# A gated cross-attention and feed-forward stack on one core: the opening stage's order of turns, key projections and GpSimd work is changed

## The chip, the cores and the metric

The kernel runs on one core of a Trainium2 chip. The time is device microseconds of one execution. A kernel's time is the median of several executions.

## The reference

`x` is 2048 tokens by 256, the context is 1601 rows by 256 with a mask. Four layers follow each other, each added to `x` behind a gate `tanh(g)`:

```python
x = x + tanh(g_xattn[0]) * latent_attention(ctx, layernorm(x), mask)   # 16 heads of 64
x = x + tanh(g_ffn[0])   * expert_ffn(layernorm(x))                    # 8 experts, top 2
x = x + tanh(g_xattn[1]) * cross_attention(layernorm(x), ctx)          # 16 heads of 16
x = x + tanh(g_ffn[1])   * quantised_ffn(layernorm(x))
```

Only the first layer's opening is touched. Its queries are `layer_norm(layernorm(x)) @ Wq`. Its keys and values come from 2048 rows of x and 1601 rows of context, one behind the other, so from 3649 keys:

```python
q = ln_lat @ Wq
k, v = split(concat([layer_norm(ctx), ln_lat]) @ Wkv)
out = softmax(q @ k.T * scale, masked) @ v            # per head
return out @ Wout
```

## The kernel before, in words

**Tiling.** `stage_latent` computes the first layer. The keys lie as 29 tiles of 128 (16 of x, 13 of context), and also as 8 chunks of 512: 4 of x, and 4 of context of which the last has 128. Two heads are worked on at once, in 8 groups. A group has 4 blocks of 512 queries. A block in a group is a unit `w`: there are 32, each of 29 steps `t`.

**Two passes over the scores.** The softmax needs a maximum per query before its scores are computed exactly. `pair(n)` is a rough pass: TensorE multiplies the high halves of 128 queries by 512 keys for two heads, and VectorE takes the two maxima (line 598). A unit has 29 such pairs. After its 29th, `max_of` makes the negated maxima, TensorE turns them (`turn`), and `shift_of` makes from them the shift that is added in `scores(w, t)`. ScalarE takes the exponential in `weigh`, TensorE multiplies by the values in `values`, and GpSimd and VectorE add up the exponentials (`add`, lines 348 and 630). Pairs run 33 ahead of the steps (`lead` = 29 + 4), so the first 33 pairs stand in an opening loop with no steps beside them. After them the loop of units interleaves `pair(n)` and `scores(w, t)`.

**The opening.** It has these parts on each engine, each written out as a program of its own and held together by semaphores:

- VectorE measures the rows of x and context (line 653), aggregates (658), makes reciprocals of deviations that ScalarE computes (line 483), and normalises: `norm_x(b)` for 4 blocks of 4 tiles of x (line 692) and `norm_ctx(b)` for the 13 tiles of context (line 699). Each signals `normed`, eight in all. Then come `project(0, a.nx)` (the low half of the first block of queries, line 565) and the loop of 33 pairs, with `fill_ctx(b)` ahead of pairs 0, 4, 8 and 12 (line 709: a transposed row block of context is scaled and masked rows are filled).
- TensorE transposes normalised rows (`turn_rows(b)`, line 826, b = 0 to 3 for x and 4 to 7 for context, two halves c each), projects (`project`, lines 845 for keys and queries, 853 for values) and computes pairs (line 885).
- ScalarE evacuates the transposes of x as full numbers and high halves (`row_block(b)`, lines 501 and 506, for context only 506), evacuates projections (lines 437, 443, 450) and rounds the steps between keys two tiles apart (`step_high`, line 462).
- GpSimd makes the low halves: of the weights (line 398), of the rows (`row_low(n)`, line 364, n = 0 to 7 for x), of the steps (`step`, `step_low`, lines 376 and 383). `fill[c]` (line 404) prepares the masked rows.

**Jobs.** There are 20 projections for a group: 8 chunks of keys, 4 blocks of queries, 8 of values. For the first group `open_jobs` gives their order. The first five (keys 0, queries 0, keys 1, 2, 3) stand before the loop of pairs, the rest behind odd pairs by `job_after_pair`. Pair n needs key chunk n // 4 for n below 28.

**Banks.** Rows and projections of the opening share four PSUM banks in turn, in the order of `open_uses`. A use waits until the fourth before it has been read:

```python
def free_open(what):
    n = open_place[what]
    if n >= 4:
        for read in open_read(open_uses[n - 4]):
            pe.wait_ge(*read)
```

For a block of queries "read" means that VectorE has made its low half. ScalarE's full rows go through three staging buffers: `row` n waits for `rows_lo` of n - 2. A projection on TensorE waits for `rows_lo` of the row blocks that it reads. `fill_ctx` waits for the same count.

Of the kernel before, what the change touches and what calls it, by code (L numbers as in the profile page):

```python
# [8 lines left out]
ACT = mybir.ActivationFunctionType  # L9
# [5 lines left out]
DC = D // P  # L15
TOK = 2048
NX = TOK // P
# [68 lines left out]
class Latent:  # L86


    def __init__(self):
        self.groups, self.heads, self.head = 8, 2, 64  # L90
        self.nl, self.nt = NX, NX + NCT
        self.keys = self.nt * P
        self.q_scale, self.gate = 0.125, 0
        self.ring = 6
        self.units = self.groups * NU
        self.steps = self.units * self.nt
        self.blocks = QB // P
        self.full = 7
        self.lead = self.nt + 4
        self.kchunks = [(a, 512) for a in range(0, NX * P, 512)] + [(NX * P + a, min(512, CTXP - a)) for a in range(0, CTXP, 512)]  # L100
        self.nx = NX * P // 512
        self.tail_at, self.tail = 1536, CTX - 1536
        self.vgroups = [list(range(a, min(a + 4, self.nt))) for a in range(0, self.nt, 4)]
        self.nk, self.nkq, self.nv = len(self.kchunks), len(self.kchunks) + NU, len(self.vgroups)
        self.jobs = self.nkq + self.nv
        keys_x, keys_c = list(range(self.nx)), list(range(self.nx + NU, self.nkq))
        queries = list(range(self.nx, self.nx + NU))
        v = list(range(self.nkq, self.jobs))
        self.open_jobs = [keys_x[0], queries[0], keys_x[1], keys_x[2], keys_x[3], v[0], v[1], keys_c[0], v[2], keys_c[1], v[3],
                          keys_c[2], keys_c[3], queries[1], v[4], queries[2], v[5], queries[3], v[6], v[7]]  # L110
        self.job_after_pair = {2 * i + 1: job for i, job in enumerate(self.open_jobs[5:19])} | {NX + NCT - 1: self.open_jobs[19]}
        self.query_low_after = {20: queries[1], 24: queries[2], 28: queries[3]}
        turns = [(0, 7), (0, 23), (0, 27), (1, 1), (1, 5), (1, 7), (1, 23), (1, 27), (2, 1), (2, 3), (2, 5), (2, 7),
                 (2, 23), (2, 27), (3, 1), (3, 3), (3, 5), (3, 7), (3, 23), (3, 27)]
        self.job_at = {((g - 1) * NU + u) * self.nt + t: (g, i) for g in range(1, self.groups) for i, (u, t) in enumerate(turns)}
        self.apart = 2
        self.sums_at, self.invert_at, self.pieces, self.divide_at, self.out_at = 9, 12, 4, 16, (17, 19)
        self.last_pair, self.turn_at = 24, 25
        self.dve_tiles = [5, 7, 9, 15, 17]
        self.pool_tiles = [t for t in range(self.nt) if t not in self.dve_tiles]  # L120


def stage_latent(nc, m, x_in, ctx_in, gates_in, affine_in, w_in, wo_in, mask_in):
# [5 lines left out]
    with Semaphores(nc, "a0") as sem, ExitStack() as ctx:  # L129
# [66 lines left out]
        order_kq = [i for i in a.open_jobs if i < a.nkq]  # L196
        turns = 2 * DC * (NL // 4)
        cols = [min(4, NL - 4 * b) * P for b in range(NL // 4)] + [min(4, NCT - 4 * b) * P for b in range(-(-NCT // 4))]
        open_uses = [("rows", n) for n in range(4)] + [("proj", 0, i) for i in a.open_jobs[0:2]]
        open_uses += [("rows", 4), ("rows", 5), ("proj", 0, a.open_jobs[2]), ("rows", 6), ("rows", 7)]  # L200
        open_uses += [("proj", 0, i) for i in a.open_jobs[3:5]]
        for n in range(a.lead):
            if n % 4 == 0 and n // 4 < turns // (2 * DC):
                open_uses += [("rows", turns // 2 + DC * (n // 4) + c) for c in range(DC)]
            if n in a.job_after_pair:
                open_uses.append(("proj", 0, a.job_after_pair[n]))
# [81 lines left out]
        def staged(n):  # L288
            return full[:, n % 3 * QB:(n % 3 + 1) * QB]
# [35 lines left out]
        def _(pool):  # L325
# [68 lines left out]
            nc.gpsimd.memset(ones[:, :], 1.0).then_inc(zeroed, 1)  # L394
            pool.wait_ge(affine_loaded, 32)
            pool.wait_ge(wscale_set, 1)
            pool.wait_ge(w_first, 1)
            nc.gpsimd.tensor_tensor(w_lo[:, :], w_st[:, :], w_hi[:, :], ALU.subtract).then_inc(w_split, 1)
            for n in range(6):
                row_low(n)  # L400
            pool.wait_ge(mask_loaded, 32)
            pool.wait_ge(affine_edge, DC)
            for c in range(DC):
                nc.gpsimd.tensor_scalar(fill[c], valid_u8[:, :], to_first[:, c:c + 1], first_key[:, c:c + 1],
                                        ALU.mult, ALU.add).then_inc(affine_edge, 1)
            row_low(6)
            row_low(7)
            for b in range(a.nk - a.nx):
                row_low(8 + 2 * b)
                row_low(9 + 2 * b)  # L410
# [19 lines left out]
        def _(act):  # L430
# [58 lines left out]
            def half_twice(h):  # L489
                act.wait_ge(var2_done, h + 1)  # L490
                deviation(var2[:, 8 * h:8 * h + 8], std[:, 8 * h:8 * h + 8])

            def row_block(b):
                for c in range(DC):
                    n = DC * b + c
                    hi, at = (m.xh, b * QB) if n < turns // 2 else (m.ch, (b - NL // 4) * QB)
                    if n < turns // 2:
                        act.wait_ge(rows_turned, n + 1)
                        if n >= 3:
                            act.wait_ge(rows_lo, n - 2)  # L500
                        nc.scalar.activation(staged(n)[:, 0:cols[b]], open_bank(("rows", n))[:, 0:cols[b]], ACT.Identity,
                                             bias=gx[:, 1, c:c + 1], scale=gx[:, 0, c:c + 1]).then_inc(full_done, 1)
                        act.wait_ge(full_done, n + 1)
                    else:
                        act.wait_ge(filled, n - turns // 2 + 1)
                    nc.scalar.activation(hi[:, c, at:at + cols[b]], staged(n)[:, 0:cols[b]], ACT.Copy).then_inc(rows_hi, 1)

            act.wait_ge(gates_loaded, 16)
            nc.scalar.activation(m.tg[:, :], gates[:, :], ACT.Tanh)
# [5 lines left out]
            nc.scalar.activation(w_hi[:, :], w_st[:, :], ACT.Copy, scale=WSCALE)  # L515
            nc.scalar.activation(w_st[:, :], w_st[:, :], ACT.Copy, scale=WSCALE).then_inc(w_first, 1)
            half(1)
            half_twice(1)
            act.wait_ge(affine_loaded, 32)
            row_block(0)  # L520
            row_block(1)
            project(0, a.open_jobs[0])
            project(0, a.open_jobs[1])
            row_block(2)
            act.wait_ge(aggregated, NT)
            deviation(mv[:, NL:NT, 1], std[:, NL:NT])
            nc.scalar.activation(warm[:, :], eps[:, :], ACT.Exp)
            project(0, a.open_jobs[2])
            row_block(3)
            project(0, a.open_jobs[3])  # L530
            project(0, a.open_jobs[4])
            for b in range(NL // 4):
                row_block(NL // 4 + b)
                if b:
                    step_high(0, b - 1)
                for n in (4 * b + 1, 4 * b + 3):
                    project(0, a.job_after_pair[n])
            step_high(0, a.nx - 1)
            for n in range(16, a.lead):
                if n in a.job_after_pair:  # L540
                    project(0, a.job_after_pair[n])
                if n in (17, 19, 21, 23):
                    step_high(0, a.nx + NU + (n - 17) // 2)
            act.wait_ge(prep, 1)
            for w in range(a.units):
                g, u = divmod(w, NU)
# [12 lines left out]
        def _(dve):  # L559
# [164 lines left out]
            aggregate(8, 8)  # L724
            norm_x(1)
            first_norm(1)
            measure_ctx(0)
            second_norm(1)
            norm_x(2)
            norm_x(3)  # L730
            for b in range(1, len(ctx_loaded)):
                measure_ctx(b)
            aggregate(NL, NCT)
# [11 lines left out]
                norm_ctx(b)  # L745
            project(0, a.nx)
            for n in range(a.lead):
                if n % 4 == 0 and n // 4 < len(ctx_loaded):
# [44 lines left out]
        def _(pe):  # L793
# [164 lines left out]

            turn_rows(0)
            turn_rows(1)  # L960
            project(0, a.open_jobs[0])
            project(0, a.open_jobs[1])
            turn_rows(2)
            project(0, a.open_jobs[2])
            turn_rows(3)
            project(0, a.open_jobs[3])
            project(0, a.open_jobs[4])
            for n in range(a.lead):
                if n % 4 == 0 and n // 4 < len(ctx_loaded):
                    turn_rows(NL // 4 + n // 4)  # L970
                if n == NT + 1:
                    turn(0)
                pair(n)
                if n in a.job_after_pair:
                    project(0, a.job_after_pair[n])
            pe.wait_ge(prep, 1)
            for w in range(a.units):
                g, u = divmod(w, NU)
                for t in range(NT):
                    n = w * NT + t + a.lead  # L980
                    if t % 2 == 0:
# [1404 lines left out]
```

## Time and profile before

| | us |
|---|---|
| median of 3 runs | 3269.82 |
| lowest and highest | 3268.73, 3271.04 |
| the profiled execution, its own time | 3268.37 |
| its span in the trace | 3266.5 |

The span lies 1.9 us below the profiled execution's own time. Over the span TensorE's matmuls are busy for 2956.8 us (91%), VectorE for 2435.5 us (75%), GpSimd for 2101.2 us (64%) and ScalarE for 1801.1 us (55%). The opening takes the first 91 us, about 3% of the span, so these shares say little about it; it has to be read from the timeline of each engine in that stretch. A duration in the timeline reaches to an instruction's end; the next one of the same engine often starts some 0.08 us before that, so a repeated cost is read from start to start.

### The profile page before, as it was taken

What the parts mean: (1) busy time and instruction counts of PE and PEld (TensorE: products, weight loads), DVE (VectorE), ACT (ScalarE), POOL (GpSimd) and SP (SyncE); (2) the same over time, 40 slices, a digit from 0 to 9 for tenths busy, and PEclk for the clock granted to TensorE, in tenths of its full rate; (3) what the DMA queues carried; (4) which work ended last, traced back from release to release, by engine and by line L of the source; (5) the groups of instructions that cost most, each with busy time, mean ns of one, the idle gap of its engine ahead of it and who ended that gap; (6) DMA issues with size and microseconds to landing.
All of it is one profiled execution on the core that took longest, in us unless ns stands there. A gap on an engine that the chain in (4) does not pass through costs nothing. (4 is left out here: it accounts for less than half of the span.)

```text
span 3266.5 us, 53578 instructions
## 1 busy us (share of the span) xinstructions
PE 2956.8 (91%) x21712; PEld 1094.2 (33%) x21720; DVE 2435.5 (75%) x3023; ACT 1801.1 (55%) x2009; POOL 2101.2 (64%) x1000
## 2 busy tenths in 40 slices
PE   5899999999999999999999999998597799999977
PEld 3233333333333333333333333322454133333334
DVE  8777787677777778767777776782545888888878
ACT  4455555455445555555554555445433488888863
POOL 5787988898898888889879888989510111111022
PEclk9999999999999999999999999999698799999989
DMA  1000000000000000000000000000210100000000
GB/s 62 6 1 1 1 8 1 1 7 1 1 7 1 1 1 7 1 1 7 1 1 1 2 1 1 1 1 1 68 32 14 43 8 7 6 7 8 5 3 25
DMA packets 24615, 28.72 MB, mean 9 GB/s; under 512 B 6511, under 2 KB 21296, under 8 KB 24370
## 3 DMA queue, kind: packets, MB, share of 16 engines
q1 hardware_dynamic: 24370, 25.31, 2.6%
q8 instruction: 172, 2.82, 0.4%
q14 instruction: 73, 0.60, 0.1%
HBM read 17.42 MB, written 2.10 MB: 6 GB/s over the span
## 5 line engine op out<-in xcount | busy, mean ns | idle before, releaser
L348 POOL TENSOR_TENSOR a_acc<-a_acc,a_prob 128x1024 f32<-128x1024 f32 x704 | 1725.3, 2451 | 297.7 <-ACT a_prob L480 216.0
L598 DVE TENSOR_REDUCE a_part_max<-wide 128x2 f32<-128x1024 f32 x880 | 1069.1, 1215 | 443.1 <-PE wide L885 442.3
L480 ACT ACTIVATE a_prob<-slot,a_mask_bias 128x1024 f32<-128x1024 f32 x928 | 986.9, 1113 | 738.6 <-PE slot L914 721.7
L929 PE MATMUL bank<-a_prob,a_val 128*64 128x512 f32 x3712 | 897.1, 605 | 2.1 <-ACT a_prob L480 2.1
L1218 ACT ACTIVATE a_prob<-slot,a_mask_bias 128x1024 f32<-128x1024 f32 x416 | 455.2, 1115 | 67.0 <-PE slot L1418 53.9
L885 PE MATMUL wide<-a_k_hi,a_q_hi 64*128 64x512 f16 (+1 forms) x2016 | 352.4, 362 | 113.8 <-DVE a_part_max L598 106.0
L1262 DVE TENSOR_REDUCE a_part_max<-wide 128x1 f32<-128x512 f32 x514 | 333.5, 684 | 37.6 <-PE wide L1406 20.8
L929 PEld LDWEIGHTS bank<-a_prob,a_val 128*64 128x64 f32 x3712 | 226.5, 136 | 394.0 <-issue 289.4
L914 PE MATMUL slot<-a_q_hi,a_k_lo 64*128 64x512 f16 x1856 | 352.4, 376 | 0.0
L914 PE MATMUL slot<-a_q_hi,a_k_step_hi 64*128 64x512 f16 x1728 | 327.9, 376 | 2.4 <-ACT a_prob L480 2.3
L914 PE MATMUL slot<-a_q_lo,a_k_step_hi 64*128 64x512 f16 x1728 | 327.7, 376 | 0.0
L885 PEld LDWEIGHTS wide<-a_k_hi,a_q_hi 64*128 64x128 f16 x2016 | 90.2, 93 | 550.2 <-DVE a_part_max L598 444.6
L1432 PE MATMUL bank<-a_prob,a_val 128*32 128x256 f32 x3328 | 262.8, 392 | 0.1
L1178 POOL TENSOR_TENSOR x_res<-a_gated,x_res 128x512 f32<-128x512 f32 x32 | 41.2, 1287 | 342.5 <-ACT a_gated L1230 342.5
L630 DVE TENSOR_TENSOR a_acc<-a_acc,a_prob 128x1024 f32<-128x1024 f32 x96 | 217.4, 2264 | 6.4 <-ACT a_prob L480 6.4
L1406 PE MATMUL wide<-a_k_op,a_q_op 48*128 48x512 f16 (+1 forms) x686 | 166.5, 355 | 36.5 <-DVE a_part_max L1262 29.0
L1262 DVE TENSOR_REDUCE a_part_max<-bank 128x1 f32<-128x512 f32 x254 | 173.6, 684 | 16.0 <-PE wide L1406 14.1
L1418 PE MATMUL slot<-a_q_op,a_k_op 64*128 64x512 f16 x832 | 160.9, 383 | 3.6 <-DMA a_q_op<-a_shift 2.3
L1166 POOL CAST a_hi<-a_y 128x512 f16<-128x512 f32 x15 | 9.2, 611 | 225.8 <-ACT a_y L1207 225.8
L636 DVE RECIPROCAL bank<-bank 128x128 f32<-128x128 f32 x128 | 120.8, 948 | 36.6 <-PE bank L937 36.6
L914 PEld LDWEIGHTS slot<-a_q_hi,a_k_lo 64*128 64x128 f16 x1856 | 90.5, 94 | 110.2 <-issue 0.5
L1406 PE MATMUL bank<-a_k_op,a_q_op 48*128 48x512 f16 (+1 forms) x338 | 109.6, 354 | 15.9 <-DVE a_part_max L1262 14.4
(397 smaller groups left out, 3274.7 us busy)
## 6 DMA issues: line engine op xcount, KB each, us to landing
a_w_staged<-in_w SPq DMA_DIRECT2D x8, 384.0 KB, 3.2
x_res<-in_x SPq DMA_DIRECT2D x4, 512.0 KB, 5.8
a_q_op<-a_hi SPq DMA_DIRECT2D x128, 16.0 KB, 1.8
out_x<-x_res SPq DMA_DIRECT2D x16, 128.0 KB, 1.7
a_k_op<-mid_k_hi SPq DMA_DIRECT2D x32, 52.0 KB, 2.2
mid_context<-in_ctxt SPq DMA_DIRECT2D x1, 1601.0 KB, 6.7
mid_w_staged<-in_w1a SPq DMA_DIRECT2D x4, 384.5 KB, 6.5
a_acc<-in_ctx SPq DMA_DIRECT2D x3, 512.0 KB, 8.4
```

Of the source, the lines that this page charges most:

```text
L348: nc.gpsimd.tensor_tensor(acc, before, prob[:, k % R, :], ALU.add).then_inc(added_p, 1)
L480: nc.scalar.activation(prob[:, k % R, :], m.slot[k % 2][:, :], ACT.Exp, bias=mbias[:, t:t + 1]).then_inc(probs_ready, 1)
L598: nc.vector.reduce_max(part_max[:, w % 2, :, j, c], pairs, AX.X).then_inc(max_used, 1)
L630: nc.vector.tensor_tensor(acc, before, prob[:, k % R, :], ALU.add).then_inc(added_v, 1)
L885: ins = nc.tensor.matmul(out, qh[g % 2][r, q0:q0 + P], src, start=True, stop=True, tile_position=(h * HALF, 0))
L914: ins = nc.tensor.matmul(score_bank(w, t, h), left, right, start=(whole and n == 0), stop=(n == len(terms) - 1), tile_position=(h * HALF, ...
L929: ins = nc.tensor.matmul(av[r, :], val[g % 2][:, t, r], prob[:, k % R, h * QB:(h + 1) * QB], start=(t == 0), stop=(t == NT - 1), tile_posi ...
L1218: nc.scalar.activation(prob[:, k % R, :], slot(("scores", w, s))[:, :], ACT.Exp, bias=mbias[:, t:t + 1]).then_inc(probs_ready, 1)
L1262: nc.vector.reduce_max(part_max[:, w % 2, 2 * z + h, j:j + 1, c], src, AX.X).then_inc(ring_used, 1)
L1406: ins = nc.tensor.matmul(bank(("max", n, h))[:, at:at + width_k], q_op[z][r, u * QB + j * P:u * QB + (j + 1) * P], k_op[g][z][r, k0:k0 + w ...
L1418: ins = nc.tensor.matmul(slot(("scores", w, s))[:, h * QB:(h + 1) * QB], k_op[g][z][r, t * P:(t + 1) * P], q_op[z][r, u * QB:(u + 1) * QB] ...
L1432: ins = nc.tensor.matmul(av[r, q], val[g][:, t, r], prob[:, (k + h // 2) % R, c0 + q.start:c0 + q.stop], start=(n == 0), stop=(n == a.halv ...
```

## The change

- TensorE turns rows 0, 1, 2 of x, projects keys 0, turns rows 3, projects queries 0, and goes to the loop. Keys 1, 2 and 3 are projected behind pairs 1, 3 and 5. The first block of context is turned and filled ahead of pair 2, the others ahead of pairs 6, 10, 14. The remaining jobs have places of their own, some behind pairs that follow each other.
- The order in which the banks are used follows. The first block of queries now has place 9 and not 5.
- ScalarE does the rows of x singly: row 0 ahead of the second square root, rows 4 and 5 around the deviation of context, rows 6 and 7 behind both first projections. It rounds steps at places of their own (`step_after`).
- GpSimd waits for `normed` 4 (all of x normalised) before its first two low halves and the low half of the weights, then makes rows 2 and 3, waits for `normed` 8 (context normalised), then does `fill` and rows 4 to 7.
- VectorE measures two tiles of the first context block where it measured four, and the other two behind `norm_x(3)`.
- In the first unit `scores(0, 0)` stands before `pair(33)` and not behind it.

```diff
+        self.job_after_pair = {1: keys_x[1], 3: keys_x[2], 5: keys_x[3], 7: keys_c[0], 9: v[0], 11: keys_c[1], 13: v[1], 14: queries[1],
+                               15: keys_c[2], 17: v[2], 18: v[3], 19: keys_c[3], 21: queries[2], 22: v[4], 23: v[5], 25: queries[3],
+                               27: v[6], 28: v[7]}
+        self.step_after = dict(zip((6, 9, 13, 16, 18, 20, 22, 24), keys_x + keys_c))
+        self.open_jobs = [keys_x[0], queries[0]] + list(self.job_after_pair.values())
+        self.query_low_after = {17: queries[1], 24: queries[2], 28: queries[3]}
...
+        open_uses = [("rows", n) for n in range(6)] + [("proj", 0, a.open_jobs[0])] + [("rows", 6), ("rows", 7)]
+        open_uses.append(("proj", 0, a.open_jobs[1]))
         for n in range(a.lead):
-            if n % 4 == 0 and n // 4 < turns // (2 * DC):
+            if n % 4 == 2 and n // 4 < turns // (2 * DC):
...
             pool.wait_ge(affine_loaded, 32)
             pool.wait_ge(wscale_set, 1)
+            pool.wait_ge(normed, NL // 4)
+            row_low(0)
+            row_low(1)
             pool.wait_ge(w_first, 1)
             nc.gpsimd.tensor_tensor(w_lo[:, :], w_st[:, :], w_hi[:, :], ALU.subtract).then_inc(w_split, 1)
-            for n in range(6):
-                row_low(n)
+            row_low(2)
+            row_low(3)
+            pool.wait_ge(normed, len(cols))
             pool.wait_ge(mask_loaded, 32)
             pool.wait_ge(affine_edge, DC)
             for c in range(DC):
                 nc.gpsimd.tensor_scalar(fill[c], valid_u8[:, :], to_first[:, c:c + 1], first_key[:, c:c + 1],
                                         ALU.mult, ALU.add).then_inc(affine_edge, 1)
-            row_low(6)
-            row_low(7)
+            for n in range(4, 8):
+                row_low(n)
...
             half(1)
+            act.wait_ge(affine_loaded, 32)
+            row(0)
             half_twice(1)
-            act.wait_ge(affine_loaded, 32)
-            row_block(0)
+            row(1)
             row_block(1)
+            row(4)
+            act.wait_ge(aggregated, NT)
+            deviation(mv[:, NL:NT, 1], std[:, NL:NT])
+            row(5)
+            nc.scalar.activation(warm[:, :], eps[:, :], ACT.Exp)
             project(0, a.open_jobs[0])
             project(0, a.open_jobs[1])
-            row_block(2)
...
             row_block(3)
...
             turn_rows(0)
             turn_rows(1)
+            turn_rows(2)
             project(0, a.open_jobs[0])
+            turn_rows(3)
             project(0, a.open_jobs[1])
-            turn_rows(2)
-            project(0, a.open_jobs[2])
-            turn_rows(3)
-            project(0, a.open_jobs[3])
-            project(0, a.open_jobs[4])
...
+                    if w == 0 and t == 0:
+                        scores(w, t)
+                        pair(n)
+                        continue
```

## Rows read from the trace of the kernel before

**Rows 1.** Busy time of each engine by stretch, with the granted clock.
```profile
22.80:24.00 1.20, 1.20 (x4) 0.46 (x3) 1.20 (x2) 0.23 (x1) 1.20 (x2) 0.50 0.00 0
39.00:46.20 7.20, 6.37 (x26) 3.76 (x27) 0.01 (x1) 4.24 (x7) 2.31 (x2) 0.70 0.00 0
46.20:91.30 45.10, 33.61 (x313) 18.69 (x311) 44.39 (x46) 18.36 (x37) 29.19 (x28) 0.96 0.02 3
1000.00:1700.00 700.00, 666.73 (x4374) 233.93 (x4372) 520.87 (x478) 366.13 (x414) 600.85 (x250) 1.00 0.01 2
```
The columns are: stretch, its length, busy time and count of PE, PEld, DVE, ACT and POOL, granted clock, DMA share, GB/s.

**Rows 2.** Waits in the first 92 us: total, times, longest.
```profile
PE slot L826 <- DVE a_q_lo L565: 10.2, 1, 10.2
DVE a_k_full L709 <- PE slot L826: 7.7, 3, 7.3
```

**Rows 3.** VectorE's timeline in the opening: start, us, then the instruction.
```profile
12.35 2.70 DVE L692 TENSOR_SCALAR a_prob<-x_res,a_mv,a_rstd 128x256 f32<-128x256 f32 x4
15.52 1.35 DVE L692 TENSOR_SCALAR a_prob<-x_res,a_mv,a_rstd 128x256 f32<-128x256 f32 x4
19.04 6.17 DVE L692 TENSOR_SCALAR a_prob<-x_res,a_mv,a_rstd 128x256 f32<-128x256 f32 x8
25.13 3.03 DVE L653 BATCH_NORM_STATS2 a_stats<-a_acc 128x6 f32<-128x256 f32 x9
28.07 0.96 DVE L658 BATCH_NORM_AGGREGATE a_mv<-a_stats 128x2 f32<-128x6 f32 x13
31.21 7.08 DVE L699 TENSOR_SCALAR a_acc<-a_acc,a_mv,a_rstd 128x256 f32<-128x256 f32 x13
38.20 0.69 DVE L565 SCALAR_TENSOR_TENSOR a_q_lo<-slot,a_q_hi 128x512 f16<-128x512 f32 x1
46.19 0.75 DVE L709 SCALAR_TENSOR_TENSOR a_k_full<-slot,a_affine_c,a_prob 128x512 f32<-128x512 f32 x1 [7.30 <-PE slot L826]
...
47.52 1.22 DVE L598 TENSOR_REDUCE a_part_max<-wide 128x2 f32<-128x1024 f32 x1
48.65 1.22 DVE L598 TENSOR_REDUCE a_part_max<-slot 128x2 f32<-128x1024 f32 x1
...
89.91 1.22 DVE L598 TENSOR_REDUCE a_part_max<-wide 128x2 f32<-128x1024 f32 x1
```

**Rows 4.** GpSimd's timeline in the opening.
```profile
12.85 1.72 POOL L398 TENSOR_TENSOR a_w_lo<-a_w_staged,a_w_hi 128x768 f16<-128x768 f32 x1 [10.72 <-ACT a_w_staged L516]
19.10 0.19 POOL L362 COPY a_first_key<-a_k_full 128x1 f32<-128x1 f32 x1 [4.53 <-ACT xt_hi L506]
...
20.89 3.52 POOL L364 TENSOR_TENSOR xt_lo<-a_k_full,xt_hi 128x512 f16<-128x512 f32 x3
28.67 1.15 POOL L364 TENSOR_TENSOR xt_lo<-a_k_full,xt_hi 128x512 f16<-128x512 f32 x1 [4.25 <-ACT xt_hi L506]
31.14 3.46 POOL L404 TENSOR_SCALAR a_prob<-a_valid_u,a_to_first,a_first_key 128x1664 f32<-128x1664 uint8 x2
79.92 0.43 POOL L383 TENSOR_TENSOR a_k_lo<-a_k_step,a_k_step_hi 128x128 f16<-128x128 f32 x1 [1.48 <-ACT a_k_step_hi L462]
```

**Rows 5.** ScalarE's timeline, one row block's start to the next.
```profile
17.62 0.76 ACT L501 ACTIVATE a_k_full<-slot,a_affine_x 128x512 f32<-128x512 f32 x1
...
18.95 0.76 ACT L501 ACTIVATE a_k_full<-slot,a_affine_x 128x512 f32<-128x512 f32 x1
```

**Rows 6.** TensorE's timeline: a cold projection's part, a warm one's, and the first scores.
```profile
23.30 1.06 PE L845 MATMUL slot<-xt_hi,a_w_lo 128*128 128x512 f16 x2
44.26 0.59 PE L845 MATMUL slot<-xt_hi,a_w_hi 128*128 128x512 f16 x2 [0.80 <-issue]
91.66 0.66 PE L914 MATMUL slot<-a_q_hi,a_k_hi 64*128 64x512 f16 x2
93.36 0.66 PE L914 MATMUL slot<-a_q_hi,a_k_hi 64*128 64x512 f16 x2
94.77 0.39 PE L885 MATMUL wide<-a_k_hi,a_q_hi 64*128 64x512 f16 x2
```

More of the change, by code:

```diff
@@ L108, in __init__ @@
         v = list(range(self.nkq, self.jobs))
[L109 to L112, printed above, removed]
+        self.job_after_pair = {1: keys_x[1], 3: keys_x[2], 5: keys_x[3], 7: keys_c[0], 9: v[0], 11: keys_c[1], 13: v[1], 14: queries[1],
[4 more added lines that the diff above has]
+        self.query_low_after = {17: queries[1], 24: queries[2], 28: queries[3]}
         turns = [(0, 7), (0, 23), (0, 27), (1, 1), (1, 5), (1, 7), (1, 23), (1, 27), (2, 1), (2, 3), (2, 5), (2, 7),
@@ L198, in stage_latent @@
         cols = [min(4, NL - 4 * b) * P for b in range(NL // 4)] + [min(4, NCT - 4 * b) * P for b in range(-(-NCT // 4))]
-        open_uses = [("rows", n) for n in range(4)] + [("proj", 0, i) for i in a.open_jobs[0:2]]
-        open_uses += [("rows", 4), ("rows", 5), ("proj", 0, a.open_jobs[2]), ("rows", 6), ("rows", 7)]
-        open_uses += [("proj", 0, i) for i in a.open_jobs[3:5]]
+        open_uses = [("rows", n) for n in range(6)] + [("proj", 0, a.open_jobs[0])] + [("rows", 6), ("rows", 7)]
+        open_uses.append(("proj", 0, a.open_jobs[1]))
         for n in range(a.lead):
-            if n % 4 == 0 and n // 4 < turns // (2 * DC):
+            if n % 4 == 2 and n // 4 < turns // (2 * DC):
                 open_uses += [("rows", turns // 2 + DC * (n // 4) + c) for c in range(DC)]
@@ L491, in half_twice, with row @@
                 deviation(var2[:, 8 * h:8 * h + 8], std[:, 8 * h:8 * h + 8])
+            def row(n):
+                b, c = divmod(n, DC)
+                hi, at = (m.xh, b * QB) if n < turns // 2 else (m.ch, (b - NL // 4) * QB)
+                if n < turns // 2:
+                    act.wait_ge(rows_turned, n + 1)
+                    if n >= 3:
+                        act.wait_ge(rows_lo, n - 2)
+                    nc.scalar.activation(staged(n)[:, 0:cols[b]], open_bank(("rows", n))[:, 0:cols[b]], ACT.Identity,
+                                         bias=gx[:, 1, c:c + 1], scale=gx[:, 0, c:c + 1]).then_inc(full_done, 1)
+                    act.wait_ge(full_done, n + 1)
+                else:
+                    act.wait_ge(filled, n - turns // 2 + 1)
+                nc.scalar.activation(hi[:, c, at:at + cols[b]], staged(n)[:, 0:cols[b]], ACT.Copy).then_inc(rows_hi, 1)
             def row_block(b):
                 for c in range(DC):
[L495 to L506, printed above, removed]
+                    row(DC * b + c)
             act.wait_ge(gates_loaded, 16)
@@ L517, in _ @@
             half(1)
+            act.wait_ge(affine_loaded, 32)
+            row(0)
             half_twice(1)
-            act.wait_ge(affine_loaded, 32)
-            row_block(0)
+            row(1)
             row_block(1)
+            row(4)
[3 more added lines that the diff above has]
+            nc.scalar.activation(warm[:, :], eps[:, :], ACT.Exp)
             project(0, a.open_jobs[0])
             project(0, a.open_jobs[1])
-            row_block(2)
-            act.wait_ge(aggregated, NT)
-            deviation(mv[:, NL:NT, 1], std[:, NL:NT])
-            nc.scalar.activation(warm[:, :], eps[:, :], ACT.Exp)
-            project(0, a.open_jobs[2])
-            row_block(3)
-            project(0, a.open_jobs[3])
-            project(0, a.open_jobs[4])
[L532 to L539, printed above, removed]
+            row_block(3)
+            for n in range(a.lead):
+                if n % 4 == 2 and n // 4 < len(ctx_loaded):
+                    row_block(NL // 4 + n // 4)
                 if n in a.job_after_pair:
                     project(0, a.job_after_pair[n])
-                if n in (17, 19, 21, 23):
-                    step_high(0, a.nx + NU + (n - 17) // 2)
+                if n in a.step_after:
+                    step_high(0, a.step_after[n])
             act.wait_ge(prep, 1)
@@ L726, in _ @@
             first_norm(1)
-            measure_ctx(0)
+            dve.wait_ge(ctx_loaded[0], 16)
+            measure(rows(0, 2), NL, 2)
             second_norm(1)
@@ L730, in _ @@
             norm_x(3)
+            measure(rows(0, 4)[:, 2:4, :], NL + 2, 2)
             for b in range(1, len(ctx_loaded)):
@@ L747, in _ @@
             for n in range(a.lead):
-                if n % 4 == 0 and n // 4 < len(ctx_loaded):
+                if n % 4 == 2 and n // 4 < len(ctx_loaded):
                     fill_ctx(n // 4)
@@ L960, in _ @@
             turn_rows(1)
+            turn_rows(2)
             project(0, a.open_jobs[0])
+            turn_rows(3)
             project(0, a.open_jobs[1])
-            turn_rows(2)
-            project(0, a.open_jobs[2])
-            turn_rows(3)
-            project(0, a.open_jobs[3])
-            project(0, a.open_jobs[4])
             for n in range(a.lead):
-                if n % 4 == 0 and n // 4 < len(ctx_loaded):
+                if n % 4 == 2 and n // 4 < len(ctx_loaded):
                     turn_rows(NL // 4 + n // 4)
```

## The prediction

> **What bounds the kernel now.** I first split the span into stretches by busy time. In steady state TensorE is busy for 667 of 700 us, but in the first 91 us it is not the bound [rows 1]. There VectorE's timeline sets the pace: one chain of normalising up to 38.9, a hole, then 33 pairs of maxima to 91.1 (the last starts at 89.91 and takes 1.22). In the stretch from 46.2 VectorE is busy for 44.4 of 45.1 us [rows 1, 3]. Everything in the units comes behind that last pair: the first scores start at 91.66 [rows 6]. So the opening's end is the date to move, and each microsecond there should move all that follows.
>
> Two things in the opening are seen to be wasted. The waits name the first: TensorE stood for 10.2 us until VectorE had made the first queries' low half at 38.9, because bank place 9 (rows 6 of x) waits for place 5, those queries. After it came the last turns of x, keys 2 and 3 and the turns of context; VectorE waited 7.3 us for those before its fill at 46.19 [rows 2, 3].
>
> The second is in VectorE's own durations. Four normalising instructions took 1.35 us at 15.52, but 2.70 at 12.35 and 6.17 for eight at 19.04; thirteen took 7.08 at 31.21 [rows 3]. The slow ones are those beside GpSimd: its weight subtract starts at 12.85, its row subtracts at 19.10, its fill of 3.46 us at 31.14 [rows 4]. Undisturbed one costs 0.32 us (1.35 less an overlap of 0.08, by four). In the last group 11 undisturbed ones leave 3.5 us for two, about 1.73 each, which is one of GpSimd's two fills (3.46 by two).
>
> **The pause of GpSimd.** The first four norms save 1.35 us and the eight of blocks 2 and 3 save 6.17 - 2.70 = 3.5. Two statistics moved behind them save another 0.65 (3.03 us for nine is 0.33 each). So norm_x(3) ends 5.5 us earlier, at 19.7 and not 25.2 [rows 3]. Its turns come in time, as the first two blocks' normalising ends earlier as well. Then VectorE has 11 statistics (3.6) and 13 aggregates (0.9): 24.2.
>
> GpSimd starts at 19.8. Rows 0 and 1 with their small copies took 20.89 - 19.10 + 1.17 = 3.0, the weights 1.7, rows 2 and 3 take 1.17 each [rows 4]: 22.8, 24.5, 26.8. ScalarE's row 4 waits for the second of these, 22.8, and takes 1.33 [rows 5], so the deviation of context behind it runs at 24.3, just in time. The few small operations before the context norms can meet GpSimd's rows 2 and 3, so I let the norms start only at 26.9. Thirteen at 0.32 to 0.33 end at 31.1 instead of 38.3: 7.2 us gained.
>
> What nothing in the trace shows is a statistic beside a GpSimd instruction; here 11 run beside it. The nearest row is the aggregates: 13 in 0.96 us, the last of them beside the subtract that starts at 28.67, with no slowing [rows 3, 4]. I take 0. The other end is that each is held as a norm is, one for each GpSimd instruction of about 1.2 us: six get through by 26.8, and the other five, the aggregates and the small operations push the norms' start by 3.3 us. A gain from below nothing is excluded, since they had no company before.
> The Trainium skill (SBUF — State Buffer, its section on what contends) says that a VectorE instruction with at most one SBUF input and outside the two-port modes does not contend with GpSimd, while one in a two-port mode is fully blocked by a GpSimd instruction that started first. By it the statistics cost 0; the 1.73 us of a blocked norm agree with the second half, and no row here shows the first half for statistics.
>
> **What the pause makes late.** The weights' low half comes at 24.5 and not 14.6, and the first projection with it. SP's load of the second group's weights stands behind that signal; those weights are used after the last opening projection, so this costs nothing. A projection of six matmuls of 512 columns costs 2.6 us at the lower clock (0.50 granted, 0.43 us for each) and 1.3 at the higher (0.22 each) [rows 1, 6]. TensorE is idle before 24.5, so keys 0 is cold: 27.1. Turns of rows 3 take it to about 28, queries 0, between the two prices, to 30.1, their high half to 30.7. VectorE's low half follows at 31.1 and ends at 31.8; even a cold projection shifts this by a microsecond that falls into the hole below. Pairs 0 and 1 take 1.13 each start to start [rows 3]: 34.1.
>
> GpSimd now does its fills only after 31.1: 34.6. Rows 4, 5, 6 follow at 35.8, 36.9 and 38.1. The first fill_ctx halves wait for the counts 6 and 7, that is 36.9 and 38.1. So VectorE gets a new hole of 2.8 us at 34.1, and the fill ends at 38.1 + 0.67 = 38.8 (0.67 from 46.19 to 47.52 for two) [rows 3, 4]. Behind the same queue ScalarE's row 7 waits for count 5 (35.8) and holds the evacuation of keys 1 until about 38; pair 4 needs it at 41. TensorE's turn of the second context half waits for row 7's full numbers (36.5), ready by 37.5. Neither ends later than GpSimd.
>
> **The pair loop.** Before, the first context fill ended at 47.5 with no pair done; now it ends at 38.8 with two. From there the loop holds the same VectorE work: 91.1 - 8.7 - 2 x 1.13 = 80.1. To be added are gaps by TensorE. It has three more projections there, and jobs behind successive pairs (13 to 15, 17 to 19, 21 to 23). With a job behind every pair its cycle is 1.3 + 0.3 for the pair against VectorE's 1.13, a deficit of 0.45 us a pair; the two banks of pairs hide part and VectorE's fills and low halves more. I take 0.3 for each of three runs and 0.6 for keys 2 and 3, which may still be cold: 1.5. Bounds: 0, and 11 jobs at 0.5, 5.5. The loop ends at 81.6, 9.5 us earlier.
>
> **Scores before pair 33.** scores(0, 0) needs the shift, ready 2.3 us before the last pair ends, and no longer waits behind pair 33. Before, scores of two steps lay between 91.66 and 94.77; now only the second does, about 1.7 us cold. The gain is 1.4 (94.77 - 93.36), at most 1.7 [rows 6].
>
> **Sum.** 9.5 + 1.4 = 10.9 us. The profiled execution took 3268.4 around a span of 3266.5; minus 10.9 that is 3257.5. The median of the runs lies 1.4 above that execution, so I forecast 3258.9.
>
> **Rivals.**
> Statistics held by GpSimd: 3.3 us of the pause's gain go back, and the fills move with it. 3262.2. For it speaks only that no row shows the case.
> TensorE late throughout the loop: gaps of 5.5 in place of 1.5 give 3262.9. For it: three runs of jobs; against it: 33.6 us of TensorE work in a stretch of 45 [rows 1].
> The gain is taken back by the first unit (a wait for the last low step, or for values, or VectorE and GpSimd meeting differently): 3269.8. The low steps ended at 80.35, 11.3 us ahead of the first scores [rows 4, 6]; they too move forward, with at least 7 us left by my count, so this speaks against it.
> Slower by the clock: TensorE is idle at 34 to 36.5 and could stay at 1.2 GHz through the loop. Its work there is 33.6 + 3.9 for the three keys = 37.5 us; doubled, the loop would run from 32 to 107, and the time would be about 3284. Cover is 12 us, so the gain is gone once 23 of the 37.5 us run at the low clock, and it is slower by 0.2% from about 30. Against it: granted 0.96 in that stretch before, though it too began after an idle time (0.70 in the 7 us ahead) [rows 1].
>
> **How the numbers follow.** The forecast has 0.79, statistics 0.06, late TensorE 0.06, taken back 0.06, the clock 0.03. Its own range is 3255 to 3262: no gaps and 1.7 for the scores give 3257.1, and 2 us each way stand for how the first unit falls in. With two rivals the range is 3254 to 3264.5. A measurement here tells about 0.2%, 6.5 us, from no change: faster needs less than 3263.3. Forecast, statistics and half of late TensorE with a little of its rest give 0.90; same 0.07; slower 0.03.
>
> **What would show it.** Norms at 0.32 us throughout blocks 0 to 3 and the last of context near 31; w_lo ending near 24.5; a hole in VectorE from about 34 to 37, with the fill released by GpSimd's rows; no wait of 10 us in TensorE for the low queries; the last pair of 33 ending near 81.6, the first scores some 2 us before it. The forecast fails if the statistics stretch, if holes of over half a microsecond stand before many pairs, or if the first unit is longer by what the opening lost.

## The result and the profile after

The changed kernel took 3258.18 us (median of 6, 3255.98 to 3260.7) beside 3270.98 us (median of 6, 3268.73 to 3274.95) for the kernel before. The ratio is 0.9962 with a 95% interval of 0.9949 to 0.9974: between 8.5 and 16.7 us faster. The profiled execution took 3259.05 us with a span of 3257.3, against 3268.37 and 3266.5 before.

VectorE's timeline in the changed opening (start, us, then the instruction) answers to [rows 3]:

```profile
12.27 1.38 DVE L694 TENSOR_SCALAR a_prob<-x_res,a_mv,a_rstd 128x256 f32<-128x256 f32 x4
17.03 2.68 DVE L694 TENSOR_SCALAR a_prob<-x_res,a_mv,a_rstd 128x256 f32<-128x256 f32 x8
19.62 3.69 DVE L655 BATCH_NORM_STATS2 a_stats<-a_acc 128x6 f32<-128x256 f32 x11
23.22 0.95 DVE L660 BATCH_NORM_AGGREGATE a_mv<-a_stats 128x2 f32<-128x6 f32 x13
...
24.29 1.20 DVE L740 CAST a_mcol<-a_mcol_u 128x13 f32<-128x13 uint8 x1
25.66 0.94 DVE L746 TENSOR_TENSOR a_rstd<-a_rstd,a_mcol 128x13 f32<-128x13 f32 x1
26.64 4.29 DVE L701 TENSOR_SCALAR a_acc<-a_acc,a_mv,a_rstd 128x256 f32<-128x256 f32 x13
30.84 0.68 DVE L567 SCALAR_TENSOR_TENSOR a_q_lo<-slot,a_q_hi 128x512 f16<-128x512 f32 x1
...
36.85 0.75 DVE L711 SCALAR_TENSOR_TENSOR a_k_full<-bank,a_affine_c,a_prob 128x512 f32<-128x512 f32 x1 [3.06 <-POOL xt_lo L365]
37.95 0.75 DVE L711 SCALAR_TENSOR_TENSOR a_k_full<-slot,a_affine_c,a_prob 128x512 f32<-128x512 f32 x1 [0.35 <-POOL xt_lo L365]
38.62 1.22 DVE L600 TENSOR_REDUCE a_part_max<-wide 128x2 f32<-128x1024 f32 x1
...
80.82 1.22 DVE L600 TENSOR_REDUCE a_part_max<-wide 128x2 f32<-128x1024 f32 x1
```

Every norm of x and context now costs 0.32 to 0.33 us from start to start; the last eight of x took 6.17 us before and take 2.68. The context norms end at 30.9 instead of 38.3. The new hole is where it was looked for, 3.06 + 0.35 us, and its releaser is GpSimd. The loop of pairs ends at 82.04 (80.82 + 1.22) instead of 91.13.

GpSimd's timeline (answers to [rows 4]) shows the two pauses and the queue that sets the hole:

```profile
22.71 1.63 POOL L402 TENSOR_TENSOR a_w_lo<-a_w_staged,a_w_hi 128x768 f16<-128x768 f32 x1
24.31 2.26 POOL L365 TENSOR_TENSOR xt_lo<-a_k_full,xt_hi 128x512 f16<-128x512 f32 x2
31.04 3.44 POOL L409 TENSOR_SCALAR a_prob<-a_valid_u,a_to_first,a_first_key 128x1664 f32<-128x1664 uint8 x2 [4.47 <-DVE a_acc L701]
34.44 4.50 POOL L365 TENSOR_TENSOR xt_lo<-a_k_full,xt_hi 128x512 f16<-128x512 f32 x4
```

TensorE's timeline (answers to [rows 6]) shows the swapped scores: the first score matmul stands at 79.92, before the last pair's maxima are out, and pair 34 at 84.20.

```profile
79.92 0.61 PE L918 MATMUL slot<-a_q_hi,a_k_hi 64*128 64x512 f16 x2
82.09 0.61 PE L889 MATMUL wide<-a_k_hi,a_q_hi 64*128 64x512 f16 x2 [0.29 <-DVE a_part_max L600]
82.50 0.63 PE L918 MATMUL slot<-a_q_hi,a_k_hi 64*128 64x512 f16 x2
84.20 0.63 PE L889 MATMUL wide<-a_k_hi,a_q_hi 64*128 64x512 f16 x2
```

To see whether the gain is passed on, I take one instruction that stands once in each unit, the negated maxima. First the third and the last of the kernel before, then those of the changed kernel:

```profile
218.40 0.21 DVE L609 TENSOR_REDUCE a_neg_max<-a_part_max 128x8 f32<-128x64 f32 x1
...
2215.88 0.22 DVE L609 TENSOR_REDUCE a_neg_max<-a_part_max 128x8 f32<-128x64 f32 x1
```

```profile
208.11 0.21 DVE L611 TENSOR_REDUCE a_neg_max<-a_part_max 128x8 f32<-128x64 f32 x1
...
2206.72 0.22 DVE L611 TENSOR_REDUCE a_neg_max<-a_part_max 128x8 f32<-128x64 f32 x1
```

The lead is 10.3 us at the third and 9.2 at the last; the spans differ by 9.2. So the opening's gain goes through the first layer nearly one to one, and in this pair of executions through the rest of the program too. That last part is not sure to a microsecond: from the last unit's negated maxima to the end of the span, where no version changes anything, the ten traces of this document took between 1047.1 and 1050.9 us (the kernel before and the changed one both 1050.6). So a difference of up to 3.8 us between single executions can come from there, and I read the experiments at the loop's end and at the units' maxima first.

### The profile page after: what moved, and what is told of

It is laid out like the page before. It is cut to its first block and busy times, and to the rows that moved or that the text cites. A ratio compares the mean times of both kernels' runs of the same rounds, so it can differ in the third digit from the quotient of the medians.

```text
span 3257.3 us, 53578 instructions
## 1 busy us (share of the span) xinstructions
PE 2957.0 (91%) x21712; PEld 1093.0 (34%) x21720; DVE 2430.7 (75%) x3023; ACT 1800.9 (55%) x2009; POOL 2099.9 (64%) x1000
## 5 line engine op out<-in xcount | busy, mean ns | idle before, releaser
L1411 PE MATMUL bank<-a_k_op,a_q_op 48*128 48x512 f16 (+1 forms) x338 | 109.8, 355 | 15.9 <-DVE a_part_max L1267 14.4
```

Source lines behind the costliest of these rows:

```text
L1411: ins = nc.tensor.matmul(bank(("max", n, h))[:, at:at + width_k], q_op[z][r, u * QB + j * P:u * QB + (j + 1) * P], k_op[g][z][r, k0:k0 + w ...
```

## The experiments

Each kernel's time is compared with the kernel before as it was run beside it ("before beside it"), in the ratio of the medians. "Loop end" is the end of the 33rd pair's maxima in the profiled execution.

| kernel | us | before beside it | ratio, 95% interval | loop end |
|---|---|---|---|---|
| before | | | | 91.13 |
| changed | 3258.18 | 3270.98 | 0.9962, 0.9949 to 0.9974 | 82.04 |
| changed, no pause | 3263.82 | 3269.02 | 0.9983, 0.9975 to 0.9992 | 87.98 |
| before, pause only | 3274.09 | 3269.02 | 1.0014, 1.0005 to 1.0023 | 94.65 |
| before, low half first | 3263.64 | 3269.02 | 0.9981, 0.9972 to 0.9990 | 87.24 |
| changed, pair 33 first | 3259.18 | 3269.02 | 0.9971, 0.9959 to 0.9982 | 82.87 |
| changed, fills on ScalarE | 3254.4 | 3270.33 | 0.9952, 0.9939 to 0.9964 | 79.24 |
| changed, second pause out | 3261.38 | 3270.33 | 0.9974, 0.9963 to 0.9984 | 85.48 |
| before, swap only | 3267.31 | 3269.44 | 0.9994, 0.9985 to 1.0003 | 92.30 |
| fills on ScalarE, jobs spaced | 3251.6 | 3269.44 | 0.9947, 0.9935 to 0.9960 | 78.14 |

**The changed kernel without the pause.**

```diff
-            pool.wait_ge(normed, NL // 4)
-            row_low(0)
-            row_low(1)
             pool.wait_ge(w_first, 1)
...
-            row_low(2)
-            row_low(3)
-            pool.wait_ge(normed, len(cols))
+            for n in range(6):
+                row_low(n)
```

> The changed kernel with GpSimd's order of before (weights' low half as soon as it can, rows 0 to 5, fill, rows 6 and 7) and both waits for the normalising taken out. Theory (the pause is worth about 4 us, because its saving of 7 us is partly given back in GpSimd's late rows): the norms take 2.7, 6.2 and 7.1 us again, the context norms end near 38.3 instead of 30.9, no hole stands before the first context fill, the loop of pairs ends near 85.9 instead of 82.0, time about 3262. Rival (the pause is worth nothing, the turns alone made the gain): the loop ends within 1 us of 82, 3258. Rival (the pause is worth all of the 7 us): 3265.

Measured: VectorE's norms, and the first context fill of this kernel:

```profile
19.32 5.19 DVE L690 TENSOR_SCALAR a_prob<-x_res,a_mv,a_rstd 128x256 f32<-128x256 f32 x8
29.91 9.48 DVE L697 TENSOR_SCALAR a_acc<-a_acc,a_mv,a_rstd 128x256 f32<-128x256 f32 x13
...
42.17 0.73 DVE L707 SCALAR_TENSOR_TENSOR a_k_full<-bank,a_affine_c,a_prob 128x512 f32<-128x512 f32 x1
```

The theory's mechanism holds, its size was short by 2 us. The context norms took 9.48 us and not 7.1, because rows 5, 6 and 7 of GpSimd also fell beside them; they ended at 39.4 and not at 30.9. The fill had no hole before it, so 3.4 us of these 8.5 are given back there. The pause is worth 5.9 us at the loop's end; the rest of the change is 3.2 us there, and it is faster than before by 0.8 to 2.5 thousandths. The first rival (the pause is worth nothing) is out. The second (all of 7 us, 3265) is not: the median of 3263.82 lies nearer to it than to the theory's 3262, and 5.9 lies nearer to 7 than to 4. Only the hole and the norms in the trace say that part of the saving goes back.

**The kernel before with the pause alone.** The same GpSimd lines as in the change, nothing else.

> The kernel before with GpSimd's two pauses and new order alone; turns, projections and ScalarE as before. Theory (the pause needs the new order of turns): the first projections start near 24.5, the deviation of context waits on ScalarE behind them until 33, context norms end near 38, the wait of TensorE for the queries' low half stays, and GpSimd's fills and rows come after it, so that the first context fill ends near 50 instead of 47.5: about 2.8 us slower than before. Rival (the saving on VectorE is a gain by itself): 4 to 7 us faster than before.

Measured: slower, by 1.6 to 7.5 us; 5.1 by the medians and 3.5 at the loop's end, where 2.8 were expected. Its norms of x were as quick as in the changed kernel (2.67 us for eight). VectorE then stood twice:

```profile
DVE a_k_full L713 <- PE slot L830: 10.0, 1, 10.0
DVE a_rstd L743 <- ACT a_std L487: 8.2, 1, 8.2
```

ScalarE's deviation of context, which the second wait is for:

```profile
33.91 0.29 ACT L487 ACTIVATE a_std<-a_mv,a_eps 128x13 f32<-128x13 f32 x1
```

The deviation of context stands behind the first projections on ScalarE, and these wait for the weights' low half. So the 5 us saved in the norms were waited away, and the first fill started at 49.72. The rival falls: a quicker VectorE was no gain by itself. Two things of the old order stood in its way, the deviation behind the projections (8.2 us) and the bank wait for the low queries (10.0 us, with GpSimd's fills and rows 4 to 7 behind the late norms). The changed kernel has neither. No run has the pause with only one of them mended, so how much each is needed for the pause to pay is argued from the waits and not shown.

**The kernel before with one instruction moved.**

```diff
+            project(0, a.nx)
             dve.wait_ge(mask_loaded, 32)
             nc.vector.tensor_scalar(mbias[:, NL:NT], mcol_u8[:, :], -1.0, -MASKED, ALU.add, ALU.mult).then_inc(prep, 1)
...
             for b in range(len(ctx_loaded)):
                 norm_ctx(b)
-            project(0, a.nx)
```

> The kernel before with one move on VectorE: the first queries' low half is made ahead of the context norms and not behind them. Theory (the 7.3 us hole was that one wait on bank place 5): TensorE turns rows 6 and 7 near 30, projects keys 2 and 3 by 39.5, the first context fill ends near 41.9 instead of 47.5, time 5.7 us below the kernel before. Rival (the hole was TensorE's and ScalarE's amount of work and not the wait): less than 2 us.

Measured: 5.4 us faster by the medians, 3.9 at the loop's end. VectorE's timeline:

```profile
28.91 0.66 DVE L565 SCALAR_TENSOR_TENSOR a_q_lo<-slot,a_q_hi 128x512 f16<-128x512 f32 x1
...
31.69 8.75 DVE L699 TENSOR_SCALAR a_acc<-a_acc,a_mv,a_rstd 128x256 f32<-128x256 f32 x13
40.78 0.75 DVE L709 SCALAR_TENSOR_TENSOR a_k_full<-slot,a_affine_c,a_prob 128x512 f32<-128x512 f32 x1 [0.34 <-PE slot L826]
...
67.92 1.23 DVE L598 TENSOR_REDUCE a_part_max<-wide 128x2 f32<-128x1024 f32 x1 [1.61 <-PE wide L885]
```

The hole of 7.3 us is down to 0.34, so it was the wait on bank place 5, whose release stood at the end of VectorE's queue. The context norms grew from 7.08 to 8.75 us, since row subtracts of GpSimd that had waited now ran beside them. The fill came 5.4 us earlier; 1.6 of that is lost again at 67.92, where VectorE waits for a pair that stands behind a projection of queries. TensorE did this projection at 1.2 GHz (granted clock 0.50 from 64.73 to 67.41, and 1.00 from 60.00 to 64.19, ahead of it).

**The swap of the first scores, both ways.** In the changed kernel the four lines of the swap were taken out; in the kernel before they were put in.

> The changed kernel with pair(33) ahead of scores(0, 0) again. Theory: the loop of pairs ends at 82.0 as before, pair 34 comes 1.5 us later, time about 1.5 us above the changed kernel. Rival (the first unit hides it): no difference, and pair 34's delay is gone by the second unit.

> The kernel before with scores(0, 0) ahead of pair(33) and nothing else. Theory (the swap is worth what the comparison of traces showed for it, 1.2 us, in any order of the opening): the loop of pairs ends at 91.1 as before, the maxima of the third unit (218.4 before) come 1.2 to 1.5 us earlier, time 1 to 1.5 us below the kernel before, too little to be sure of by the times. Rival (its effect lies in how the clock rises in the changed opening): the third unit's maxima within 0.3 us of 218.4.

Measured: the times can't settle it (3259.18 with 3269.02 beside it, 3258.18 with 3270.98 beside it; 0.9994 with an interval over 1). The openings of two executions also differ by about a microsecond with nothing changed ahead of the swap (82.04 and 82.87; 91.13 and 92.30), so the sign that was expected, the date of the third unit's negated maxima, came out at 0.5 us in the kernel before with the swap. I read the stretch from the loop's end to these maxima in place of it, a choice made after the result. The third unit's rows, first without the swap in the changed kernel, then with it in the kernel before:

```profile
210.44 0.21 DVE L611 TENSOR_REDUCE a_neg_max<-a_part_max 128x8 f32<-128x64 f32 x1
```

```profile
217.90 0.21 DVE L609 TENSOR_REDUCE a_neg_max<-a_part_max 128x8 f32<-128x64 f32 x1
```

The stretch is 127.3 us in the kernel before (218.40 - 91.13) and 125.6 with the swap; it is 126.1 in the changed kernel and 127.6 without the swap. That is 1.5 to 1.7 us, but not all of it is the swap. The stretch in all ten traces, beside TensorE's granted clock in the first 8 us behind the loop's end:

| kernel | swap | granted clock | stretch |
|---|---|---|---|
| fills on ScalarE, jobs spaced | yes | 1.00 | 125.4 |
| before, swap only | yes | 0.96 | 125.6 |
| changed, no pause | yes | 0.92 | 125.6 |
| changed | yes | 0.79 | 126.1 |
| changed, fills on ScalarE | yes | 0.54 | 127.4 |
| changed, second pause out | yes | 0.51 | 127.6 |
| before | no | 0.79 | 127.3 |
| changed, pair 33 first | no | 0.75 | 127.6 |
| before, low half first | no | 0.73 | 127.7 |
| before, pause only | no | 0.71 | 127.8 |

With the swap the stretch runs from 125.4 to 127.6 us and follows the clock. At the same clock, 0.79, it is 126.1 with the swap and 127.3 without: by this one pair of traces the swap itself is worth 1.2 us, and the other 0.3 to 0.5 us of both comparisons go with a higher clock. So the rival of the clock fits in part, and the other one, that the first unit hides the swap, is out: pair 33 first is still 2.3 us behind the changed kernel at the last unit's maxima (2209.01 and 2206.72). Its span is as short all the same, 3257.0 against 3257.3, because its later layers took 2.6 us less.

**The second pause taken out.** Only `pool.wait_ge(normed, len(cols))` is removed from the changed kernel.

> The changed kernel without GpSimd's second pause (it no longer waits for the context norms before its fills; the first pause and the order stay). Theory (a norm beside a GpSimd instruction is held until that ends, one for each): two norms of 1.7 us, three of 1.2, the context norms end near 36.3 instead of 30.9, no hole follows, the first context fill ends near 40.6 instead of 38.6: 2 us slower than the changed kernel. Rival (the fills taken off the chain are worth more than the slower norms): 1 to 2 us faster.

Measured: 3.4 us later at the loop's end (expected 2). VectorE's norms and GpSimd beside them:

```profile
26.71 10.45 DVE L700 TENSOR_SCALAR a_acc<-a_acc,a_mv,a_rstd 128x256 f32<-128x256 f32 x13
...
39.94 0.73 DVE L710 SCALAR_TENSOR_TENSOR a_k_full<-bank,a_affine_c,a_prob 128x512 f32<-128x512 f32 x1
```

```profile
26.63 3.47 POOL L408 TENSOR_SCALAR a_prob<-a_valid_u,a_to_first,a_first_key 128x1664 f32<-128x1664 uint8 x2
30.06 4.68 POOL L365 TENSOR_TENSOR xt_lo<-a_k_full,xt_hi 128x512 f16<-128x512 f32 x4
```

GpSimd had six instructions beside the norms and not five. Seven free norms at 0.33 and six that last as long as GpSimd's instructions (3.47 + 4.68 = 8.15) give 10.5, which is the 10.45 measured. Waiting is right here: the second pause costs GpSimd about 4.5 us and saves VectorE 6.2.

**The fills moved to ScalarE.**

```diff
+            def fill_one(c):
+                act.wait_ge(mask_loaded, 32)
+                act.wait_ge(affine_edge, DC)
+                nc.scalar.activation(fill[c], valid_u8[:, :], ACT.Identity, bias=first_key[:, c:c + 1],
+                                     scale=to_first[:, c:c + 1]).then_inc(affine_edge, 1)
...
+            fill_one(0)
             row(5)
...
-            row_block(3)
+            row(6)
+            fill_one(1)
+            row(7)
```

> The changed kernel with both fills of masked rows made by ScalarE (one ahead of row 5, one ahead of row 7) and not by GpSimd; nothing else is moved. Theory (GpSimd's queue behind the context norms sets the hole of 3.1 + 0.35 us before the first context fill): rows 4 to 6 of GpSimd end near 34.5 instead of 37.95, the first context fill ends near 35.2 instead of 38.6, the loop ends near 79 instead of 82.0, time about 3 us below the changed kernel. Rival (ScalarE or TensorE sets it: row 7, the evacuation of keys 1, cold keys 2): the hole moves behind pair 3 and less than 1 us is gained.

Measured, ScalarE's two fills and then VectorE's first context fill:

```profile
24.46 1.76 ACT L510 ACTIVATE a_prob<-a_valid_u,a_first_key,a_to_first 128x1664 f32<-128x1664 uint8 x1
...
31.98 1.76 ACT L510 ACTIVATE a_prob<-a_valid_u,a_first_key,a_to_first 128x1664 f32<-128x1664 uint8 x1
```

```profile
33.75 0.74 DVE L715 SCALAR_TENSOR_TENSOR a_k_full<-bank,a_affine_c,a_prob 128x512 f32<-128x512 f32 x1
35.16 0.75 DVE L715 SCALAR_TENSOR_TENSOR a_k_full<-slot,a_affine_c,a_prob 128x512 f32<-128x512 f32 x1 [0.66 <-PE slot L834]
```

The hole shrinks to 0.66 us, the loop ends 2.8 us earlier than in the changed kernel. GpSimd's queue behind the context norms did set it. At the third unit's maxima only 1.5 us of the 2.8 are left (206.62 against 208.11), since TensorE stayed at the lower clock for longer behind the loop (0.54 against 0.79). Against the kernel before beside it this one is 15.9 us faster, the changed kernel 12.8; the intervals of the two ratios overlap. The spans differ by 5.2 us, of which 3.5 fall behind the last unit's maxima and are not owed to the fills.

**Jobs spaced.** On top of ScalarE's fills:

```diff
-        self.job_after_pair = {1: keys_x[1], 3: keys_x[2], 5: keys_x[3], 7: keys_c[0], 9: v[0], 11: keys_c[1], 13: v[1], 14: queries[1],
-                               15: keys_c[2], 17: v[2], 18: v[3], 19: keys_c[3], 21: queries[2], 22: v[4], 23: v[5], 25: queries[3],
+        self.job_after_pair = {1: keys_x[1], 3: keys_x[2], 5: keys_x[3], 7: keys_c[0], 9: v[0], 11: keys_c[1], 13: v[1],
+                               15: keys_c[2], 16: keys_c[3], 17: queries[1], 18: v[2], 19: v[3], 21: queries[2], 22: v[4], 23: v[5], 25: queries[3],
-        self.query_low_after = {17: queries[1], 24: queries[2], 28: queries[3]}
+        self.query_low_after = {18: queries[1], 23: queries[2], 28: queries[3]}
```

> The kernel with ScalarE's fills, and the run of jobs behind pairs 13, 14, 15 undone: the short keys 7 behind pair 16, queries 1, values 2 and 3 behind 17, 18, 19; low halves of queries 1 and 2 behind pairs 18 and 23. Theory (full jobs behind successive pairs make VectorE wait, 0.39 + 0.50 us in the first run and 0.54 + 0.54 in the third): the first run's 0.9 us go, the low halves inside the other runs cover part of the rest, the loop ends 1 to 1.5 us earlier than with ScalarE's fills alone. Rival (the gaps only move to the next run): within 0.3 us.

Measured: the loop ends 1.1 us earlier. The waits of VectorE on the pairs of the changed kernel (with ScalarE's fills they are the same four, 0.39, 0.50, 0.54 and 0.54 us), and of this one:

```profile
57.50 1.23 DVE L600 TENSOR_REDUCE a_part_max<-slot 128x2 f32<-128x1024 f32 x1 [0.39 <-PE slot L889]
59.22 1.23 DVE L600 TENSOR_REDUCE a_part_max<-wide 128x2 f32<-128x1024 f32 x1 [0.50 <-PE wide L889]
...
68.51 1.23 DVE L600 TENSOR_REDUCE a_part_max<-slot 128x2 f32<-128x1024 f32 x1 [0.54 <-PE slot L889]
70.28 1.23 DVE L600 TENSOR_REDUCE a_part_max<-wide 128x2 f32<-128x1024 f32 x1 [0.54 <-PE wide L889]
```

```profile
61.50 1.23 DVE L604 TENSOR_REDUCE a_part_max<-wide 128x2 f32<-128x1024 f32 x1 [0.54 <-PE wide L893]
...
65.21 1.23 DVE L604 TENSOR_REDUCE a_part_max<-slot 128x2 f32<-128x1024 f32 x1 [0.22 <-PE slot L893]
```

The waits fall from 1.97 to 0.76 us. In the last run, where the low half now stands between its jobs, 1.08 us become 0.22; in the run of 17 to 19 a new wait of 0.54 appears, so the rival is right for part of it. At the third unit the lead over ScalarE's fills alone is 3.1 us (203.56 against 206.62) and not 1.1: here TensorE's granted clock was 1.00 behind the loop, there 0.54. By the ratio this is the best version, 3251.6 us. That it beats the changed kernel rests on the traces, 3.9 us at the loop's end and 4.5 at the third unit; the intervals of the two ratios (0.9947 and 0.9962) overlap.

## Why the prediction was right

The forecast was 3258.9, measured 3258.18. The steps were right in the main, but that the two numbers lie 0.7 us apart is partly luck. The forecast took 10.9 us off, and the two profiled executions differ by 9.3, so it took off 1.6 too much. It then added 1.4 us because the median of before lay that much above its profiled execution; the changed kernel's median lies 0.9 below its own, which is 2.3 us the other way. By its steps:

- **The bound.** The opening's end is the date that counts: 10.3 us of lead at the third unit are 9.2 at the last. The 7.3 us hole was the wait for the low queries, as the run with one instruction moved shows.
- **The pause.** Norms to 19.7 forecast, 19.71 measured; context norms at 26.9 and 31.1, measured 26.64 and 30.93.
- **The statistics beside GpSimd.** I took 0: 11 took 3.69 us, 0.33 each as without company. That rival is out. By the Trainium skill (SBUF — State Buffer, "Who interferes with whom") a VectorE instruction with at most one SBUF input and outside the two-port modes does not contend with GpSimd, and one in a two-port mode is blocked. The section does not list statistics; the trace agrees with the first half if they are outside those modes, and with the second in the norms.
- **What the pause makes late.** Keys 0 were projected cold from 24.50 to 27.0, as forecast; queries 0 were warm and done at 29.6 and not 30.1. The first context fill ended at 38.6, forecast 38.8.
- **The gaps in the loop.** Beyond those of before I took 1.5 us: 0.9 for three runs of jobs and 0.6 for keys 2 and 3. From the end of the first context fill to the loop's end, two pairs taken off before, it took 41.35 us and now takes 43.42: 2.1 us. The sum is near, its parts are not. The waits stand in the runs at 13 to 15 (0.89 us) and 21 to 23 (1.08), none in 17 to 19, where a low half falls inside the run and the last job is the short one. Keys 2 did run at 1.2 GHz, but pair 4 started only 0.08 us late by it. Also, keys 1 was projected at 30.79, ahead of this stretch, so it held two more projections than before and not the three of the forecast.
- **The scores.** Pair 34 stood 3.64 us behind the loop's end and now 2.16: 1.5 us, forecast 1.4. At the third unit 1.2 are left; these two traces have the same granted clock behind the loop (0.79), so none of it is the clock's.
- **The sum.** Forecast 9.5 + 1.4 = 10.9; the trace has 9.1 + 1.2 = 10.3 at the third unit, and 9.2 at the end.

What the forecast did not have is the last 1.1 us. The lead falls in small steps, at units 9, 11, 17 (counted from 0) and 30, each about 0.3. One can be followed on VectorE, before and then changed, at the same place of the kernel:

```profile
667.08 1.58 DVE L630 TENSOR_TENSOR a_acc<-a_prob 128x1024 f32<-128x1024 f32 x1
...
670.05 1.11 DVE L587 TENSOR_TENSOR a_k_lo<-a_k_step,a_k_step_hi 128x256 f16<-128x256 f32 x1
```

```profile
656.78 1.86 DVE L632 TENSOR_TENSOR a_acc<-a_prob 128x1024 f32<-128x1024 f32 x1
...
659.75 1.39 DVE L589 TENSOR_TENSOR a_k_lo<-a_k_step,a_k_step_hi 128x256 f16<-128x256 f32 x1
```

Both are longer by 0.28 us beside a GpSimd add, the pair behind them is late by that and TensorE waits 0.18 us for it. The length of the lead is not the cause. The steps at 9, 11 and 17 stand at the same units, each of 0.2 to 0.4 us, in the changed kernel with pair 33 first, in the one without the second pause, and in the kernel before with the pause alone, whose loop ended 3.5 us later than before. Both kernels with ScalarE's fills have steps as well, part of them at other units. The three that keep GpSimd's old order (no pause, low half first, swap only) have none there. So the steps go with GpSimd's new order in the opening; by what path it reaches units hundreds of microseconds later stays open. It also stays open how much of the 12.8 us between the medians is more than the profiled 9.3: single executions of the changed kernel spread over 4.7 us.

## What to carry to other kernels

Look for an engine's own instructions that take several times their usual duration: here 0.33 us became about 1.2 to 1.8 beside GpSimd, and no wait in the profile showed it. Letting GpSimd pause pays when the idle engine's work afterwards is short or can be given to a third engine, and only once the other waits of that stretch are out of the way: the same pause made the old order slower. Compare stretches at the same granted clock before a microsecond is put down to an edit: of the 1.5 to 1.7 us that the swap seemed to be worth, about 1.2 were its own. In a ring of banks, a use whose release stands late in another engine's queue holds everything behind it, so such a release belongs further ahead, as the run with one instruction moved shows; placing the use at the ring's end, as the change does, was not run alone.

## What the runs showed of the hardware

Beside GpSimd a row normalisation of VectorE (128x256, SBUF to SBUF) lasted about as long as the GpSimd instruction, one for each. With the second pause out, 6 of 13 did, and the thirteen took 10.45 us in place of 4.29. Operations on 128x13 were held too: a cast took 1.20 us in the changed kernel and 0.16 in the kernel before, a product of two tensors 0.94, and 0.17 in the run without the pause, where GpSimd stood idle at that moment. GpSimd lost little by it: four row subtracts took 4.50 us alone and 4.68 beside the norms.

Statistics, aggregates and maxima from PSUM did not change (0.33, 0.07 and 1.13 us from start to start). A fill of 128x1664 from uint8 took ScalarE 1.76 us and GpSimd 1.72, and ScalarE had room for both fills.

The granted clock of TensorE was 0.50 (1.2 GHz) from 24.5 to 27.0 in the changed kernel, after 4.9 us without a matmul, and 1.00 (2.4 GHz) when queries 0 were projected from 28.1 on. TensorE then stood idle from 32.7 to 36.5. The two pairs at 37.1 still ran at 2.4 GHz (0.39 us for two matmuls); keys 2, begun at 37.6, ran at 1.2 GHz (1.06 us for two, granted clock 0.52 from 37.6 to 40.3). Behind the loop of pairs the granted clock over 8 us lay anywhere between 0.51 and 1.00 in the ten traces, and with the swap in place the stretch from there to the third unit's maxima took 2.2 us more at the low end than at the high one.
